# Attention of an adaLN block in 64x64 parts of the array, with one 192-key strip for 64 queries, transposes of 64 rows, and the output in the score banks

## The reference

```python
# light attention: a window of 64 queries sees its own and both neighbouring windows
q, k, v = split(layernorm(x) @ wqkv_l, 3)
sim  = einsum('bhnid,bhnjd->bhnij', qw * scale, kk)      # 64 queries x 192 keys
sim  = where(valid, sim, neg)                            # the first and last window have 128
lo   = einsum('bhnij,bhnjd->bhnid', softmax(sim), vv)
light_out = lo @ wo_l
# heavy attention: 256 routed queries on 256 routed keys, chosen by sorting x @ rt
hattn = softmax(einsum('bhid,bhjd->bhij', hq * scale, hk))
heavy_out = scatter(einsum('bhij,bhjd->bhid', hattn, hv) @ wo_h)
# around it: adaLN modulation of the input, gates, a residual, and an MLP with
# squared relu whose output drives a spiking neuron of five steps
```

## Time and profile before

| | us |
|---|---|
| median of three runs | 988.05 |
| lowest and highest | 985.18, 989.50 |
| the profiled execution | 984.39 |
| its span | 982.7 |
| one pass of the loop | 110.4 |
| mean granted TensorE clock | 0.969 of full |

### The profile page before, as it was taken

The page is one execution under the profiler, slowest core; times in us unless marked ns, Lnnn a source line. Parts: engine busy times, 40 slices in busy tenths (PEclk is TensorE's granted clock), DMA queues, the critical chain, the costliest instruction groups (busy, mean ns, idle before and its releaser), DMA issues.

```text
span 982.7 us, 19077 instructions
## 1 busy us (share of the span) xinstructions
PE 879.1 (89%) x6866; PEld 674.1 (69%) x6866; DVE 552.5 (56%) x1556; ACT 617.0 (63%) x1682; POOL 402.6 (41%) x453
## 2 busy tenths in 40 slices
PE   5759689899998999899999999899999999999655
PEld 2436567678766877678766877678766877688455
DVE  7645644764557454764557464764557454613344
ACT  1167666676567766676567766676567766777332
POOL 4422040364525453364525453365525443252333
PEclk7989899999999999999999999999999999999968
DMA  9120002100220012200220012200220011200100
GB/s 320 67 81 1 25 31 70 60 1 13 68 84 23 1 39 86 59 2 12 74 79 22 2 38 87 60 2 12 76 76 23 2 38 55 60 2 1 39 22 22
DMA packets 32461, 45.06 MB, mean 46 GB/s; under 512 B 3928, under 2 KB 26720, under 8 KB 32368
## 3 DMA queue, kind: packets, MB, share of 16 engines
q1 hardware_dynamic: 26944, 31.24, 9.9%
q0 software_dynamic: 4608, 12.59, 3.9%
q10 hardware_dynamic: 816, 0.00, 0.0%
HBM read 28.85 MB, written 14.97 MB: 45 GB/s over the span
## 4 chain that ended last, share of the span: by engine, by line
PE 64%; DVE 21%; ACT 6%; issue 4%; POOL 2%; DMA 2%; SPq 1%; DVEq 0%; POOLq 0%; ACTq 0%
PE ps_unit L889 25%; PE ps_y L1000 9%; PE ps_oT L1069 7%; PE ps_unit L937 6%; PE ps_pT L1045 5%; PE ps_scores L1033 4%; PE ps_scores L1025 3%; DVE row_min L1289 3%; PE ps_unit L942 3%; ACT probs L828 3%; DVE late L1215 1%; DVE hT L1318 1%; DVE bn L1251 1%; ACT hT L792 1%; DVE hn L1264 1%
## 5 line engine op out<-in xcount | busy, mean ns | idle before, releaser
L828 ACT ACTIVATE probs<-ps_scores,row_min 128x256 f32<-128x256 f32 (+1 forms) x384 | 171.9, 453 | 133.7 <-DVE row_min L1289 133.6
L839 ACT ACTIVATE probs<-probs,row_inv 128x256 f32<-128x256 f32 (+1 forms) x384 | 166.1, 485 | 0.0
L846 ACT ACTIVATE probsT<-ps_pT 128x512 f32<-128x512 f32 x192 | 113.5, 591 | 41.7 <-PE ps_oT L1069 41.7
L1289 DVE TENSOR_REDUCE row_min<-ps_scores 128x2 f32<-128x384 f32 (+1 forms) x192 | 122.3, 637 | 23.6 <-PE ps_scores L1033 10.8
L1045 PE MATMUL ps_pT<-ident,probs 128*128 128x128 f32 x768 | 116.4, 274 | 3.1 <-ACT probsT L846 2.9
L889 PE MATMUL ps_unit<-xT,wfcT 128*128 128x512 f32 (+1 forms) x432 | 106.1, 386 | 7.3 <-DVE xT L1230 6.7
L889 PE MATMUL ps_unit<-xT,wqkv 128*128 128x512 f32 x384 | 108.6, 419 | 4.0 <-POOL xT L651 4.0
L1300 DVE COPY loT<-ps_oT 128x128 f32<-128x128 f32 x128 | 36.3, 283 | 132.2 <-PE ps_oT L1069 132.2
L428 POOL TENSOR_TENSOR hid<-hid 128x512 f32<-128x512 f32 (+1 forms) x64 | 63.3, 989 | 107.9 <-ACT hid L805 106.9
L1045 PEld LDWEIGHTS ps_pT<-ident,probs 128*128 128x128 f32 x768 | 93.0, 141 | 19.3 <-issue 3.5
L1000 PEld LDWEIGHTS ps_y<-wprojT,hid_parts 128*128 128x128 f32 x768 | 99.8, 191 | 9.1 <-issue 5.2
(11 more groups left out here) (157 smaller groups left out, 1508.6 us busy)
## 6 DMA issues: line engine op xcount, KB each, us to landing
xa<-in_L_attn_x SPq DMA_DIRECT2D x8, 512.0 KB, 4.9
routed<-sorted_rows SPq DMA_DIRECT2D x16, 256.0 KB, 2.9
lx<-in_L_attn_x SPq DMA_DIRECT2D x8, 512.0 KB, 3.9
out_x<-spikes SPq DMA_DIRECT2D x16, 256.0 KB, 2.9
routed_out<-late SPq DMA_DIRECT2D x8, 256.0 KB, 2.1
full<-mod_rows SPq DMA_DIRECT2D x7, 256.0 KB, 5.0
sorted_rows<-hn,rank POOLq DMA_INDIRECT x64, 2.4
gate_a<-mod_rows SPq DMA_DIRECT2D x8, 128.0 KB, 3.5
```

The lines of the kernel that those rows point to most:

```text
L828: ins = act.activation(probs[:, probs_buffer(s), h * SEL + lo:h * SEL + hi], ps_scores[:, h, base + lo:base + hi], ACT.Exp, bias=row_min[: ...
L839: ins = act.activation(part, part, ACT.Identity, scale=row_inv[:, s % 3, h:h + 1])
L846: act.activation(probsT[:, :], ps_pT[:, :], ACT.Copy).then_inc(pT_copied, 1)
L1289: dve.tensor_reduce(row_min[:, s % 3, :], ps_scores[:, :, base + lo:base + hi], AX.X, ALU.min).then_inc(min_ready, 1)
```

## The change

- Light scores: a window of 64 queries now has one strip of 192 keys, columns 0 to 191, in bank `w`; the head lies in the partition half `c = h ^ w`. No columns are masked, and the mask constant and its writes go. The first window of tile 0 and the second of tile 3 have 128 keys.
- Heavy scores: four 64x64 matmuls with 256 keys, in columns 0 to 255 of the same banks.
- `minimum` reads 2x192 columns in one operation, or two operations where the halves differ (tiles 0 and 3). `exp_step` and `normalize` work on a bank each, with 192, 128 or 256 columns.
- `turn`: six (light) or eight (heavy) transposes of 64 rows by 128 columns against a 64x64 identity, alternating between the row halves `c`, into `ps_turned`, two banks. `copy_pT` copies 384 or 512 columns, reordered.
- `attend`: all matmuls 64x64. The row half `g` of the keys writes bank `g ^ h`, so each bank holds one part of the sum over keys. Light: four matmuls with 128 columns (both windows) and two to four with 64 (the neighbour tile). Heavy: eight with 128. The result lies in columns 256 to 383 of the score banks.
- `copy_out` adds the two banks (`tensor_reduce` over pairs) instead of a copy.
- New waits, since output and scores share banks: attend(n) waits for exp_step(n + 3), and copy_out(n) for scores(n + 4).
- V is projected from plain tiles of xT; the ring columns and their small operations on VectorE (L1226) and POOL (L649) go.

```diff
-def score_columns(s):
+def score_columns(s, part):
     if s >= LIGHT:
         return 0, SEL
     m = s % T
-    return (W if m == 0 else 0), (SEL - W if m == T - 1 else SEL)
+    return (W if m == 0 and part == 0 else 0), (2 * W if m == T - 1 and part == 1 else 3 * W)
+
+def probs_columns(s, part):
+    lo, hi = score_columns(s, part)
+    first = part * SEL if s >= LIGHT else (1 - part) * 3 * W
+    return slice(first + lo, first + hi)
...
-        ps_pT = ctx.enter_context(nc.psum_tensor("ps_pT", [P, 512], F32))
-        ps_oT = ctx.enter_context(nc.psum_tensor("ps_oT", [P, 512], F32))
+        ps_oT = ps_scores[:, :, SEL:SEL + P]
+        ps_turned = ctx.enter_context(nc.psum_tensor("ps_turned", [P, 2, 512], F32))
+        ps_pT = ps_turned[:, :, 0:SEL]
...
-                pool.tensor_tensor(xT_ring[1][:, k, 0:W], full[:, k, N - W:N], xT_ring[0][:, k, 0:W].bitcast(F32),
-                                   ALU.subtract)
...
-                act.activation(probsT[:, :], ps_pT[:, :], ACT.Copy).then_inc(pT_copied, 1)
+                if s < LIGHT:
+                    act.activation(probsT[:, 0:6 * W].rearrange("p (i c n) -> p c i n", i=3, c=2),
+                                   ps_pT[:, :, 0:3 * W].rearrange("p c (i n) -> p c i n", i=3),
+                                   ACT.Copy).then_inc(pT_copied, 1)
+                else:
+                    act.activation(probsT[:, :].rearrange("p (c n) -> p c n", c=2), ps_pT,
+                                   ACT.Copy).then_inc(pT_copied, 1)
...
-                    for w, h in ((0, 0), (1, 1), (1, 0), (0, 1)):
-                        lo = W if m == 0 or w == 1 else 0
-                        hi = SEL - W if m == T - 1 or w == 0 else SEL
-                        first_key, query = m * P - W + lo, m * P + w * W
-                        ins = pe.matmul(ps_scores[w * W:(w + 1) * W, h, lo:hi],
+                    for h, c in ((0, 0), (1, 1), (1, 0), (0, 1)):
+                        w = h ^ c
+                        lo, hi = score_columns(s, w)
+                        first_key, query = m * P + (w - 1) * W, m * P + w * W
+                        ins = pe.matmul(ps_scores[c * W:(c + 1) * W, w, lo:hi],
...
-                for t in range(2):
-                    for h in range(2):
-                        ins = pe.transpose(ps_pT[:, (2 * t + h) * P:(2 * t + h + 1) * P],
-                                           probs[:, probs_buffer(s), h * SEL + t * P:h * SEL + (t + 1) * P],
-                                           ident[:, :])
+                for i in range(3 if s < LIGHT else 4):
+                    for c in range(2):
+                        run = (i - 1) % 3 if s < LIGHT else i ^ 2 * c
+                        rows = slice(c * W, (c + 1) * W)
+                        ins = pe.transpose(ps_pT[:, c, i * W:(i + 1) * W],
+                                           probs[rows, probs_buffer(s), run * P:(run + 1) * P], ident[rows, rows])
...
                 pe.wait_ge(pT_copied, n + 1)
-                if not (isinstance(n, int) and n == 0):
+                if n > 0:
                     pe.wait_ge(oT_copied, n)
+                pe.wait_ge(exp_ready, min(n + 4, SLOTS * B))
...
+                    for g, h in ((0, 0), (1, 1), (1, 0), (0, 1)):
+                        both = probsT[halves[g], h * W:h * W + 2 * (3 - 2 * h) * W].rearrange(
+                            "p (w n) -> p w n", w=2)[:, :, 0:W]
+                        ins = pe.matmul(ps_oT[halves[h], g ^ h, :], v[halves[g], m, cols[h]], both,
+                                        start=True, stop=m == (T - 1, 0)[g])
+                    for g, h in ((0, 0), (1, 1), (1, 0), (0, 1)):
+                        if m != (T - 1, 0)[g]:
+                            w = 1 - g
+                            ins = pe.matmul(ps_oT[halves[h], g ^ h, w * W:(w + 1) * W], v[halves[g], m + 1 - 2 * g, cols[h]],
+                                            turned[halves[g], 2, h ^ w, :], start=False, stop=True)
...
-                for t in range(2):
-                    for h in range(2):
-                        c0 = p * P + h * DH
-                        ins = pe.matmul(ps_oT[h * DH:(h + 1) * DH, 0:P], values[t][:, c0:c0 + DH],
-                                        probsT[:, (2 * t + h) * P:(2 * t + h + 1) * P],
-                                        start=(t == 0), stop=(t == 1))
+                    for t in range(2):
+                        for g, h in ((0, 0), (1, 1), (1, 0), (0, 1)):
+                            ins = pe.matmul(ps_oT[halves[h], g ^ h, :], v_r[halves[g], t, cols[h]],
+                                            turned[halves[g], 2 * h + t, :, :], start=(t == 0), stop=(t == 1))
...
-                dve.tensor_reduce(row_min[:, s % 3, :], ps_scores[:, :, base + lo:base + hi], AX.X,
-                                  ALU.min).then_inc(min_ready, 1)
+                (lo, hi), other = score_columns(s, 0), score_columns(s, 1)
+                if (lo, hi) == other:
+                    ins = dve.tensor_reduce(row_min[:, s % 3, :], ps_scores[:, :, lo:hi], AX.X, ALU.min)
+                else:
+                    dve.tensor_reduce(row_min[:, s % 3, 0:1], ps_scores[:, 0, lo:hi], AX.X, ALU.min)
...
                 dve.wait_ge(oT_ready, n + 1)
+                dve.wait_ge(scores_ready, min(n + 5, SLOTS * B))
...
-                dve.tensor_copy(dst[:, p, m * P:(m + 1) * P], ps_oT[:, 0:P]).then_inc(oT_copied, 1)
+                dve.tensor_reduce(dst[:, p, m * P:(m + 1) * P], ps_oT.rearrange("p g n -> p n g"), AX.X,
+                                  ALU.add).then_inc(oT_copied, 1)
...
-            dve.memset(ps_scores[0:W, :, SEL - W:SEL], MASKED).then_inc(masks_made, 1)
-            dve.memset(ps_scores[W:P, :, 0:W], MASKED).then_inc(masks_made, 1)
```

More of the change, by code:

```diff
@@ L53 @@
 BANKS = 2
-MASKED = 3.0e38
 SLOT_UNITS = {
@@ L240, in adaln_block_kernel @@
         full = sb("full", [P, 2, N])
-        xT_ring = [sb(f"xT{i}", [P, KD, W + N], F32R) for i in range(2)]
-        xT = [t[:, :, W:W + N] for t in xT_ring]
+        xT = [sb(f"xT{i}", [P, KD, N], F32R) for i in range(2)]
         rank = sb("rank", [P, 2, T], I32)
@@ L835, in normalize @@
                 act.wait_ge(inv_ready, n + 1)
-                lo, hi = score_columns(s)
-                for h in range(2):
-                    part = probs[:, probs_buffer(s), h * SEL + lo:h * SEL + hi]
-                    ins = act.activation(part, part, ACT.Identity, scale=row_inv[:, s % 3, h:h + 1])
+                for part in range(2):
+                    rows = probs[:, probs_buffer(s), probs_columns(s, part)]
+                    ins = act.activation(rows, rows, ACT.Identity, scale=row_inv[:, s % 3, part:part + 1])
                 ins.then_inc(probs_ready, 1)
@@ L1007, in scores @@
             def scores(segment, b, n, s):
-                if isinstance(n, int) and n == 0:
-                    pe.wait_ge(masks_made, 2)
-                else:
+                if n > 0:
                     pe.wait_ge(exp_ready, n)
@@ L1031, in scores @@
                         wait_drained(pe, segment, b, ("HQ", p // 2), ("HK", p // 2))
-                    for h in range(2):
-                        ins = pe.matmul(ps_scores[:, h, SEL:2 * SEL], qT_r[heads[h], p, j * P:(j + 1) * P],
-                                        kT_r[heads[h], p, :], start=True, stop=True)
+                    for h, c in ((0, 0), (1, 1), (1, 0), (0, 1)):
+                        query = j * P + c * W
+                        ins = pe.matmul(ps_scores[c * W:(c + 1) * W, h ^ c, 0:SEL],
+                                        qT_r[heads[h], p, query:query + W], kT_r[heads[h], p, :],
+                                        start=True, stop=True)
                 ins.then_inc(scores_ready, 1)
@@ L1072, in attend @@
+                    cols = [slice(p * P + h * DH, p * P + (h + 1) * DH) for h in range(2)]
+                    for t in range(2):
+                        for g, h in ((0, 0), (1, 1), (1, 0), (0, 1)):
+                            ins = pe.matmul(ps_oT[halves[h], g ^ h, :], v_r[halves[g], t, cols[h]],
+                                            turned[halves[g], 2 * h + t, :, :], start=(t == 0), stop=(t == 1))
                 ins.then_inc(oT_ready, 1)
```

34 lines of the change are left out of this document (17 added, 17 removed).

## The result

| | before | after |
|---|---|---|
| median of 20 runs | 987.5 us (985.2 to 990.1) | 995.8 us (986.7 to 1003.1) |
| ratio | | 1.0075, 95% interval 1.0054 to 1.0097 |
| profiled execution, span | 984.4, 982.7 us | 1000.9, 999.1 us |
| granted clock, mean | 0.969 | 0.930 |

A forecast was written before the change was run, and what follows sets the result against it. TensorE was taken to bound two thirds of a pass, VectorE and ScalarE chains the first third. Six passes at -3.0 us (-18), last batch -4, first -2, start -0.7 summed to -24.7, giving 963 us, range 945 to 992.

The forecast's parts named there:

- rival 1: VectorE's sum over two banks dearer than 0.41 us: up to 0.78, 975 to 988 us, chance 0.09; beyond, 0.05.
- 2: TensorE's transposes: each pair costs 0.11 us, 2.5 us a pass, 982 us in all; chance 0.12.
- 3: TensorE's transposes: each alone keeps 0.11 us, 7.6 us a pass, 1020 us in all; chance 0.07.
- 4: Joint of attend and scores: the pause stays despite both being 64x64, +15 us, 978 in all; chance 0.07.
- Rival 6: Scores and attend: row halves writing one bank are held, phases stream twice, over 80 us, 1040 in all; chance 0.04.
- rival 5: Granted clock falls around one gap, at most 1.7 us, seven times, 12 us, 975 in all; chance 0.06.
- (a): Slots 0 to 8, chain to the HO projection, which waits for copy_out of slot 23: +0.3 us.
- (b): Slots 0 to 8, chain from HO to HV: one copy longer, +0.15 us.
- (c): Slots 0 to 8, chain from HV to FC: attend held, copy later and longer, +0.6 us.
- (d): Slots 0 to 8, behind FC's start: one slot's saving, -0.38 us.
- Heavy slots: TensorE in heavy slots: -0.26 us each, seven from slot 17 to the scores in slot 0, -1.8 a pass.
- The ends: Outside the six loop passes: first batch -2 us, last batch -4, start -0.7.

The follow-up runs named there:

- e14: e9 run again unaltered (after with dummy matmuls ahead of the three clock falls): 979.7 us, ratio 0.991 against before.
- e16: e9 with the slot 16 dummies written to the other bank of the turned probabilities: 977.4 us, ratio 0.989 against before.
- e15: e4 run again unaltered (after with light transposes of 128 rows): 982.6 us, ratio 0.993 against before.
- e4: After with the light slots' six 64-row transposes as three of 128 rows, heavy ones kept at 64: 982.8 us, ratio 0.992 against before.
- e1: After with attend's output beside the turned probabilities, so without both added waits; copy_pT waits for the earlier copy_out instead: 977.4 us, ratio 0.988 against before.
- e5: After with e1 and e4 together, output beside the turned probabilities and light transposes of 128 rows: 969.2 us, ratio 0.979 against before.
- e3: Before with the two added waits and nothing else, all shapes as before: 1010.1 us, ratio 1.023 against before.
- e18: e3 run again unaltered (before with the two added waits): 1014.2 us, ratio 1.025 against before.
- e11: Before, unaltered, run again as a control: 987.7 us, ratio 1.000 against before.
- e10: e6 with the 64-row transposes kept, that is e1 plus e6's dummy matmuls: 966.0 us, ratio 0.975 against before.
- e6: e5 plus dummy matmuls: four ahead of HO, ten ahead of the second Z3, four ahead of FC: 964.0 us, ratio 0.9745 against before.
- e2: After plus dummy matmuls in TensorE's idle stretches: ahead of HO, FC, the second Z3 and four attends: 998.1 us, ratio 1.0085 against before.
- e9: After plus dummy matmuls only ahead of the three places where the clock falls (HO, FC, slot 16's attends): 987.1 us, ratio 0.997 against before.
- e17: e6 run again unaltered: 964.4 us, ratio 0.974 against before.

## Why the prediction was wrong

**What held.** The light slot lost 0.38 by forecast and 0.35 to 0.40 by the periods from transposes to transposes (4.96 to 4.61, 4.54 to 4.17); the middle third 2.3 and 2.25; the sum over two banks 0.41 and 0.42:

```profile
L1323 DVE TENSOR_REDUCE loT<-ps_scores 128x128 f32<-128x256 f32 x128 | 53.5, 418 | 141.3 <-PE ps_scores L1029 92.0
```

That disposes of rival 1. Six transposes within 0.40 us and the attend 0.34 behind their start dispose of 2 and 3: within a slot the three pairs start at 444.77, 444.88 and 444.94, the later step 0.06 us. The distance from attend to scores, 0.38 us for 0.59, disposes of 4. Rival 6 is gone as well: scores of both row halves write one bank, and eight records lie within 0.51 us. The Trainium skill (TensorEngine Tiling (Array Packing), Restrictions and Gotchas) says that different row tiles can't access one bank at once; here they do, in different partitions of it, at no cost that the trace shows.

**The step that failed: rival 5, the clock.** The mechanism was named, with a chance of 0.06 and a price of one fall a pass, 1.7 us, 12 us in all. It is what happened, and more of it: three falls a pass, of 1.7, 1.4 and 1.5 us. Taken away (e14, e16), after goes from 995.8 to 979.7 and 977.4 us: 16 to 18 us, with 0.4 us a pass of dummies still in it. The low chance came from reading one place: I took the emptiest stretch of before, 1.58 busy of 3.4 us at full clock, as proof of room below. But the stretches ahead of the falls of after have 1.80 to 1.88, more than that, and in its first loop pass two such stretches (1.83 and 1.81) brought no fall. The profile's busy share doesn't order them. The low price came from looking at one gap, not at the three places where a block of full-size matmuls follows a gap.

The small shapes have a part in it. With light transposes of 128 rows the stretches ahead of HO and FC look the same (e15, 1.81 and 1.80 busy, HO's gap 1.59 us), even the number of records is near (30 for 34, 31 for 34), and the clock stays up there in all passes of e4 and e15:

```profile
389.20:392.60 3.40, 1.81 (x30) 1.25 (x29) 2.30 (x7) 2.06 (x7) 0.00 (x0) 1.00 0.00 0
418.75:422.15 3.40, 1.80 (x31) 1.29 (x31) 2.68 (x10) 1.96 (x5) 2.18 (x6) 1.00 0.02 5
```

The transposes ahead of slot 17 are heavy ones, which e4 and e15 leave at 64 rows, and there the clock still falls, in two and in five passes of six:

```profile
463.01 0.46 PE L1056 MATMUL ps_turned<-ident,probs 64*128 64x64 f32 x8
464.49 0.71 PE L1077 MATMUL ps_scores<-probsT,v 64*64 64x128 f32 x8 [1.02 <-ACT probs L829]
```

The gaps that the added waits lengthen have the other part, but not everywhere. The falls in the six loop passes of each trace:

| falls | HO, slot 1 | FC, slot 8 | slot 17 | elsewhere |
|---|---|---|---|---|
| after: small transposes, added waits | 5 | 5 | 6 | 0 |
| e4, e15: light transposes of 128 rows | 0, 0 | 0, 0 | 2, 5 | 1, 1 |
| e1: without the added waits | 0 | 6, at double length | 0 | 0 |
| e5: both undone | 0 | 4, two at double length | 2 | 0 |
| e3: before with the waits | 0 | 0 | 1 | 0 |

At HO undoing either takes the fall away. At FC the old transposes do so only while the waits stay. Without them nothing holds TensorE up earlier, it waits longer before the second Z3 (1.98 us for 1.55), and the stretch there has 1.42 us busy of 3.4. By what measure shapes and gaps bring the clock down, no run here shows.

**The waits, mis-sized.** Forecast for slots 1 to 8: +0.7 us. In the pass of after without a fall there (the first of the loop), it is 35.44 for 34.30: +1.14. By the prediction's parts: (a) to HO +0.35 for +0.3; (b) to HV +0.06 for +0.15; (c) to FC +0.74 for +0.6, with three attends late by 1.0 to 1.1 us where the sum had priced one. What is left is (d): one slot's saving behind FC's start. Slot 8's own saving went into the wait ahead of FC, 1.00 for 0.64 us, and the next one is already among the six of slots 9 to 14. I had counted it twice.

On the old shapes the waits were further off. The prediction's terms for them come to about 1 us a pass (the 995 us of e18's expectation), and e3 has 2.7: +0.33 in slot 1, 0.2 and 0.77 in 4 and 5, 0.09 and 0.39 in 6 and 7, 0.64 in 17, 0.31 in 24. Up to 1.0 us of it, in slots 4 and 5, may be the late signals; the other 1.8 us are not, since none stand there.

**Heavy slots, mis-sized.** Forecast -0.26 each; measured 4.97 to 4.75, -0.21; seven of them in sum -1.2, not -1.8, since the last three gain 0.19, 0.19 and lose 0.05 (in slot 24 the waits take 0.31 in e3, and I had priced them at nothing there). Slots 15 to 17 come to -0.04 without the fall.

A pass without falls is then 1.14 - 2.24 - 0.04 - 1.18 = -2.3 us against the forecast -3.0, and e15's one pass without a fall has 108.03 for 110.35.

**The ends.** I gave the first batch -2, the last -4 and the start -0.7. From the starts of the transposes:

| us | start | first batch | six passes | last batch | rest |
|---|---|---|---|---|---|
| before | 62.2 | 104.5 | 662.2 | 92.5 | 61.2 |
| before again (e11) | 62.6 | 107.1 | 663.2 | 92.4 | 63.8 |
| after | 63.3 | 106.3 | 672.7 | 92.7 | 64.2 |
| after, clock kept (e16) | 62.4 | 107.0 | 652.6 | 92.0 | 64.6 |

Nothing of the 6.7 us is there but 0.5 in the last batch: the clock falls at the ends in every trace, and two executions of before differ there by 5 us.

So the forecast was -24.7 us. The passes gain 4 us less and the ends 6 less, which leaves about -14. With the clock kept up the gain is 10 us (e16), and 2.4 us of dummies are against it. The clock then takes 18 back, and after stands at +8.

**Sharing banks** costs about 13 us that the change doesn't need: with the output beside the turned probabilities the same is computed, and with dummies this takes 966.0 us (e10), or 964.0 with light transposes of 128 rows (e6), 2.5% below before.

## What to carry to other kernels

Price a clock fall at every place where a long block of matmuls follows a wait, not at the emptiest one, and don't read the busy share of one stretch as room for another when the shapes change. A change that makes TensorE's work shorter ahead of a wait can lose more there than it gains; a few dummy matmuls in that wait show whether it did, if the block behind them is timed and not only the whole kernel: e2 and e9 had the blocks short and the total still long. And when an edit shares a buffer to save space, look whether the copy and the next producer, now in one line, sit on the chain that feeds the waiting engine: here that cost about 13 us of the 24 by which e6 is below before.

## What the runs showed of the hardware

- The clock fell behind stretches with 1.80 to 1.88 us busy of 3.4 in after, and held behind ones with 1.58 in before and 1.81 in e15. The light transposes, and the copy that reads them, are all that differs between after and e15, and neither the busy share nor the number of records (34 and 30) shows the difference.
- TensorE's semaphore events came late, by some 2 us at most, in the traces of e1 to e10, e17 and e18, and not in those of e11 to e16, taken between them. One chip had both. It cost e9 7 us (987.1 and 979.7), and e4 about 1 us a pass, hidden in its total by fewer falls (982.8 and 982.6). The kernel before, run beside them, was 988.8 to 990.4 us where they had it, 987.8 and 988.2 where not. The cause isn't known. A total compared across the two groups can be 7 us off.
- Score matmuls from two row halves into one bank, in different partitions, run side by side: eight records in 0.51 us.
